# Spectral mixing with the weights as stationary 32-column tiles and a block-diagonal spectrum moving, and an inverse height transform in four 32-row tiles

## The reference

```python
xf = jnp.fft.rfft2(x, norm='forward')
w1 = jax.lax.complex(w1_real, w1_imag)
w2 = jax.lax.complex(w2_real, w2_imag)
top = jnp.einsum('bixy,ioxy->boxy', xf[:, :, :hm0, :hm1], w1)
bot = jnp.einsum('bixy,ioxy->boxy', xf[:, :, -hm0:, :hm1], w2)
out_fft = out_fft.at[:, :, :hm0, :hm1].set(top)
out_fft = out_fft.at[:, :, -hm0:, :hm1].set(bot)
return jnp.fft.irfft2(out_fft, s=(h, w), norm='forward')
```

## Time and profile before

| | |
|---|---|
| median of 3 runs | 598.17 us (598.06 to 601.45) |
| the profiled execution | 597.12 us, its span 595.3 us |
| PE busy | 552.4 us (93%), 9988 matmuls and 9988 weight loads |
| DVE, ACT, POOL busy | 346.0 (58%), 302.6 (51%), 115.1 us (19%) |
| mean granted clock of PE | 0.966 of full speed |
| transfers | 41.55 MB, 27.49 MB read from HBM |

### The profile page before, as it was taken

One profiled execution on the slowest core, in us unless ns is written; L12 is line 12 of the kernel. 1 busy time (PEld: TensorE's weight loads), 2 busy tenths in 40 slices (PEclk: granted clock), 3 DMA queues, 4 the chain that ended last, 5 costly groups with the idle time before them and its releaser, 6 DMA issues.

```text
span 595.3 us, 22931 instructions
## 1 busy us (share of the span) xinstructions
PE 552.4 (93%) x9988; PEld 500.4 (84%) x9988; DVE 346.0 (58%) x813; ACT 302.6 (51%) x838; POOL 115.1 (19%) x240
## 2 busy tenths in 40 slices
PE   8988988999999899986999999979999999987997
PEld 8978888999998797686999988868999999986873
DVE  3657989544435953784555445435555554568726
ACT  4546989553348610364444444424445777667200
POOL 4000000000016000000333333473332034372000
PEclk9999989999999797997999999979999999998979
DMA  9830765060000000000000012340000144600007
GB/s 354 350 141 2 284 233 196 2 254 30 1 2 1 2 2 20 0 2 1 4 4 3 5 26 70 98 101 4 4 4 4 26 78 76 107 10 1 2 3 282
DMA packets 50251, 41.55 MB, mean 70 GB/s; under 512 B 44998, under 2 KB 45126, under 8 KB 48934
## 3 DMA queue, kind: packets, MB, share of 16 engines
q1 hardware_dynamic: 49304, 38.51, 20.0%
q0 software_dynamic: 704, 1.18, 0.9%
q10 hardware_dynamic: 144, 0.39, 0.2%
HBM read 27.49 MB, written 4.19 MB: 53 GB/s over the span
## 4 chain that ended last, share of the span: by engine, by line
PE 75%; DVE 14%; POOL 4%; ACT 4%; issue 2%; DMA 0%; SPq 0%; POOLq 0%; DVEq 0%; ACTq 0%
PE PS L739 39%; DVE RB L971 5%; PE PS L708 5%; PE PS L473 4%; PE PS L658 3%; PE PS L602 2%; PE PS L572 2%; PE PS L551 2%; PE PS L558 2%; PE PS L452 2%; PE PS L527 2%; POOL RCD L393 2%; POOL RE L390 2%; PE PS L632 2%; PE PS L482 2%
## 5 line engine op out<-in xcount | busy, mean ns | idle before, releaser
L739 PE MATMUL PS<-RE,conv_sb 128*64 128x64 f32 x6048 | 231.2, 230 | 4.4 <-DVE RE L1109 4.0
L739 PEld LDWEIGHTS PS<-RE,conv_sb 128*64 128x64 f32 x6048 | 209.9, 139 | 25.7 <-DVE RE L1109 4.7
L864 ACT COPY PS<-convb_sb 128x64 f32<-128x64 f32 x504 | 108.2, 215 | 112.9 <-DVE RE L1121 98.8
L1121 DVE SCALAR_TENSOR_TENSOR RE<-PS,RCD 128x64 f32<-128x64 f32 x252 | 56.7, 225 | 58.1 <-PE PS L739 50.0
L402 POOL COPY RCD<-RE 128x128 f32<-128x128 f32 x126 | 37.0, 294 | 156.3 <-DVE RE L1121 156.2
L1121 DVE SCALAR_TENSOR_TENSOR RE<-PS,RE 128x64 f32<-128x64 f32 x126 | 32.7, 259 | 28.3 <-PE PS L739 25.9
L802 ACT COPY RB<-PS 32x256 f32<-32x256 f32 x64 | 42.3, 661 | 6.9 <-PE PS L511 6.2
L971 DVE COPY RB<-PS 32x256 f32<-32x256 f32 x64 | 42.1, 658 | 5.2 <-PE PS L511 4.3
L1121 DVE SCALAR_TENSOR_TENSOR RE<-PS,RB 128x64 f32<-128x64 f32 x126 | 28.4, 225 | 28.1 <-PE PS L739 28.1
L527 PE MATMUL PS<-RE,RB 128*64 128x64 f32 x1024 | 32.5, 224 | 7.7 <-DVE RCD L980 3.7
L473 PE MATMUL PS<-warm 128*128 128x128 bf16 x468 | 35.5, 244 | 3.9 <-DVE warm L892 1.4
(11 more groups left out here) (118 smaller groups left out, 769.6 us busy)
## 6 DMA issues: line engine op xcount, KB each, us to landing
RE<-wspec SPq DMA_DIRECT2D x8, 2048.0 KB, 8.9
RA<-x_in SPq DMA_DIRECT2D x8, 512.0 KB, 7.5
RCD<-x_in SPq DMA_DIRECT2D x1, 4096.0 KB, 13.4
out<-RA SPq DMA_DIRECT2D x8, 512.0 KB, 2.7
RCD<-RB SPq DMA_DIRECT2D x58, 64.0 KB, 2.6
RE<-RCD SPq DMA_DIRECT2D x32, 80.0 KB, 2.4
conv_sb<-conv_w SPq DMA_DIRECT2D x1, 768.0 KB, 20.0
w_sb<-w SPq DMA_DIRECT2D x2, 264.0 KB
```

Source lines behind the costliest of these rows:

```text
L739: m = pe.matmul(conv_bank(s, u, c)[o:o + OC], conv_sb[:, s, d, o:o + OC], prev, start=False, stop=(d == 2), skip_group_check=True)
L864: act.copy(banks_of, convb_sb[:, s:s + 1].unsqueeze(2).to_broadcast([P, c1 - c0, n])).then_inc(s_seed, 1)
L1121: dve.scalar_tensor_tensor(out=state[:, state_slot(s, u), b0:b1, 1:1 + HO], in0=conv_bank(s, u, c), scalar=0.0, in1=row_at(SRC[s], s, q, u ...
```

## The change

The roles in `mix` are exchanged. The weights are now stationary: for every kx and for real and imaginary part (w) a tile of 128 rows (4 ky x 32 input channels) and 32 columns (output channels). The spectrum moves: XB holds for each kx three planes of 32 columns (minus imaginary, real, imaginary), block-diagonal over the four ky, and a matmul takes two neighbouring planes, 64 columns. The two matmuls of a kx add up in PSUM, so that the complex product comes out whole. Four kx go to four column tiles (j), PSUM partitions 32 j. A chunk has 128 matmuls where it had 64. Two banks hold a chunk's result where four did, and they alternate between chunks; DVE drains one, ACT the other, into V in RC. The two slots of XB lie in RB and RD; POOL zeroes 6144 columns of each, the second after six groups of `dft_w` have read RD.

`spread` on each engine has for two ky a copy of 32 x 1024 and a negated one of 32 x 512. Imtmp, the turning of separate products, the subtraction and addition are gone; 64 transposes turn V into VT in RA, drained by ACT and DVE in turn. `dft_h` works on 32 rows (16 of kx, real and imaginary) in four row tiles, one for each ky (q), each into its own bank, and adds over four j: 256 matmuls of 32 x 128 by 128 in four groups, where there were 64 of 128 x 128. Its table `inv_h` becomes a parameter of its own (128 x 4 x 128, in the last 512 columns of RB), loaded as an eighth one. The drains of `dft_h` alternate between DVE and ACT. The copies after the first transposes write RA in another order, and the weights are packed otherwise, in the same 2 MB per chunk. The reload of x waits for the 64 transposes.

The core of the diff:

```diff
-WCOLS = 2 * X8 * KYC * 2 * C
+XCOLS = H * 3 * KYC * B
+WCOLS = H * 2 * C
@@ sync
+            sp.dma_start(inv_h, invh).then_inc(s_par, 16)
...
-                    sp.wait_ge(s_mix, 4 * (c - 2))
+                    sp.wait_ge(s_mix, 2 * (c - 2))
...
-            sp.wait_ge(s_t0, NCH)
-            sp.wait_ge(s_t1, NCH)
+            sp.wait_ge(s_pt, NCH)
             sp.dma_start(RC, x_in).then_inc(s_xr, 16)
@@ gpsimd
-            pool.memset(RB[:, :], 0.0).then_inc(s_zero, 1)
+            pool.memset(RB[:, 0:XCOLS], 0.0).then_inc(s_zero, 1)
+            pool.wait_ge(s_ff, XCOLS // 1024)
+            pool.memset(RD[:, 0:XCOLS], 0.0).then_inc(s_zero, 1)
@@ tensor, mix
-                for k in range(4):
-                    if c >= 1:
-                        pe.wait_ge(s_md if k < 2 else s_ma, 2 * (c - 1) + k % 2 + 1)
+                for k in range(2):
+                    if c >= 2:
+                        pe.wait_ge(s_ma if k else s_md, c - 1)
                     for n in range(8):
...
-                            m = pe.matmul(o[:, x % 2, y],
-                                          XB[:, c % 2, x, 2 * y + a].rearrange("p r q b -> p (r q b)"),
-                                          WR[:, c % 3, a, x, y, :], start=True, stop=True)
+                        for w in range(2):
+                            for j in range(4):
+                                x = 4 * (8 * k + n) + j
+                                m = pe.matmul(PS[C * j:C * j + C, 4 + 2 * (c % 2) + k, 64 * n:64 * n + 64], WR[:, c % 3, x, w, :],
+                                              XB[c % 2][:, x, 1 - w:3 - w].rearrange("p r q b -> p (r q b)"),
+                                              start=(w == 0), stop=(w == 1))
@@ tensor, after the mixing
+                for b in range(B):
+                    m = pe.transpose(blk(product_slot(c), b), V_of_b[:, c, :, b], ident)
+                m.then_inc(s_pt, 1)
+            def dft_h(i):
+                pe.wait_ge(s_pta, 3 if i == 0 else 4)
+                pe.wait_ge(s_ptd, 3 if i == 0 else 4)
+                if i >= 2:
+                    pe.wait_ge(s_dra if i % 2 else s_drd, 1)
+                for c in range(4):
+                    for j in range(4):
+                        for q in range(KYC):
+                            rows = slice(C * q, C * q + C)
+                            m = pe.matmul(blk(PS[:, 4 * (i % 2) + q, :], c), VT[rows, i // 2, 4 * (i % 2) + c, j],
+                                          inv_h[rows, j, :], start=(j == 0), stop=(j == 3))
+                m.then_inc(s_df, 1)
@@ vector, spread (ACT the same for q = 2, 3)
-                for o, i in xb_pairs(c, 0):
-                    m = dve.tensor_copy(o, i)
+                for q in (0, 1):
+                    (o, i), (o_neg, i_im) = xb_pairs(c, q)
+                    dve.tensor_copy(o, i)
+                    m = dve.tensor_scalar(o_neg, i_im, -1.0, None, ALU.mult)
```

More of the change, by code:

```diff
@@ L27 @@
 NCH = KY // KYC
-X8 = H // 2 // Q
-WCOLS = 2 * X8 * KYC * 2 * C
+KXH = H // 4
+XCOLS = H * 3 * KYC * B
+WCOLS = H * 2 * C
 NF = BH * TOK
@@ L38, with build_kernel @@
 AX_X = mybir.AxisListType.X
-def build_kernel(nc, x_in, dft, wspec, conv_w, conv_b, gate_w, gate_b, w1, w2, b2, own, out):
+def build_kernel(nc, x_in, dft, invh, wspec, conv_w, conv_b, gate_w, gate_b, w1, w2, b2, own, out):
     with ExitStack() as ctx:
@@ L197, in t1_pairs @@
             g = j - G_T1
[L198 to L223, removed]
+            o = RA[:, :].rearrange("p (t b k c) -> p t b k c", t=BH, b=BL, k=KY)[:, g // 4, :, 8 * (g % 4):8 * (g % 4) + 8]
@@ L508, in spectrum @@
                     pe.wait_ge(s_xba, c - 1)
-                for bh in range(BH):
-                    for y in range(KYC):
-                        m = pe.matmul(blk(PS[:, 2 * (c % 2) + bh, :], y), blk(RA, bh * KY + c * KYC + y), fwd_h,
-                                      start=True, stop=True)
+                for b in range(B):
+                    m = pe.matmul(blk(banks(2 * (c % 2), 2), b), blk(RA, b * NCH + c), fwd_h, start=True, stop=True)
                 m.then_inc(s_f2, 1)
@@ L796, in spread @@
                 act.wait_ge(s_f2, c + 1)
-                if c == 0:
-                    act.wait_ge(s_zero, 1)
-                if c >= 2:
-                    act.wait_ge(s_mix, 4 * (c - 1))
-                for o, i in xb_pairs(c, 2):
-                    m = act.copy(o, i)
+                if c < 2:
+                    act.wait_ge(s_zero, c + 1)
+                else:
+                    act.wait_ge(s_mix, 2 * (c - 1))
+                for q in (2, 3):
+                    (o, i), (o_neg, i_im) = xb_pairs(c, q)
+                    act.copy(o, i)
+                    m = act.activation(o_neg, i_im, ACT.Copy, scale=-1.0)
                 m.then_inc(s_xba, 1)
@@ L808, in _ @@
                     spread(c + 1)
-                for k in (2, 3):
-                    act.wait_ge(s_mix, 4 * c + k + 1)
-                    act.copy(z_bank(c, k), PS[:, 4 + k, :]).then_inc(s_ma, 1)
-            for c in range(NCH):
-                act.wait_ge(s_t1, c + 1)
-                if c >= 2:
-                    act.wait_ge(s_comb, c - 1)
-                act.copy(imtmp[:, c % 2, :], banks(4 * (c % 2) + 2, 2)).then_inc(s_tmp, 1)
-            for first, pairs in ((0, t2_pairs), (8, t3_pairs)):
-                for g in range(8):
-                    act.wait_ge(s_tf, first + g + 1)
-                    for o, i in pairs(g):
-                        m = act.copy(o, i)
-                    m.then_inc(s_td, 1)
+                act.wait_ge(s_mix, 2 * c + 2)
+                o, i = z_pair(c, 1)
+                act.copy(o, i).then_inc(s_ma, 1)
+            for c in range(0, NCH, 2):
+                act.wait_ge(s_pt, c + 1)
+                o, i = t2_pair(c)
+                act.copy(o, i).then_inc(s_pta, 1)
+            for n in (1, 3):
+                act.wait_ge(s_df, n + 1)
+                for o, i in if2_pairs(n):
+                    m = act.copy(o, i)
+                m.then_inc(s_dra, 1)
+            for g in range(8):
+                act.wait_ge(s_tf, g + 1)
+                for o, i in t3_pairs(g):
+                    m = act.copy(o, i)
+                m.then_inc(s_td, 1)
             def experts(l):
```

138 lines of the change are left out of this document (56 added, 82 removed).

## The result

The kernel after takes 608.6 us (median of 4 runs, 607.34 to 612.9) against 598.3 us (4 runs, 598.06 to 601.45): 2.0% slower, the ratio 1.0204 with a 95% interval of 1.0153 to 1.0254. The forecast was 605.5 us. The profiled execution took 609.57 us, its span 607.8; for before these are 597.12 and 595.3, a difference of 12.45 us.

The account below looks back on a forecast made before the run. DVE's spread bounded the mixing before, PE the time after it; after the change PE's instruction supply would bind. Mixing ending at 128.8, then 7.1, 14.8 + 2.5 and 3.1 put L602 at 156.3: +8.3 on 597.1, 605.5 us; 8-in-10 range 588 to 629.

Parts of the forecast that it names:

- DVE bound the mixing and is freed: Mixing stage: DVE's spread copies and drains set the pace at 6.6 us a chunk; the change cuts them to 4.5 us.
- the third that I gave as a sign: Mixing stage, sign that the forecast is right: DVE stands idle for a third of the stage.
- Start of the mixing: First spread ends after 3.8 us, at 55.8 us, and mixing starts there instead of at 57.36.
- Four column tiles quarter a pass: Mixing matmuls: two tiles halve a pass, so four were taken to quarter it, to 14.5 ns, 3.7 us for 256.
- rival of tiles that gain nothing beyond two: Mixing passes stay at 31 ns: 614 us, or 628 us if row tiles too go only by twos; together chance 0.28.
- The program sets the pace: Mixing: instruction pieces arrive every 3.5 us, later behind loads; 10.5 us a loaded chunk (bounds 5.9 and 12.4), 73 us in all.
- 2 to 4 as the sign: Mixing, sign that the forecast is right: PE gaps marked issue of 2 to 4 us, always 254 visible instructions apart.
- the second rival: Mixing: running loads don't matter, pieces come every 3.5 us, mixing ends at 113.8; 590 us, chance 0.15.
- Transposes: After the mixing: 64 transposes at 0.11 us each take 7.1 us, to 135.9, with their drains hidden.
- Inverse transform over the height: 512 passes at 29 ns on four row tiles, 14.8 us, plus 2.5 for a piece made late by the reload of x.
- Tail: After the height transform: the last group's two ACT copies and first turned one stay exposed, 3.1 us, before L602 starts.
- The rival of a program that arrives in time: Mixing and after: PE runs at its own pace without waiting for instructions, 24 us earlier; 573 us, chance 0.17.

## Why the prediction was right, and by how much it was off

The forecast was +8.3 us at the first L591; the profiles show 160.18 - 147.96 = 12.2, and 0.3 after it. Step by step:

- **DVE bound the mixing and is freed.** Right: copies of 1.21 and 0.67 us and a drain of 0.69, against 1.23, 0.69 and 0.69 forecast. Its share of the chain falls from 58.8% (L971 and L980) to 0.8%. DVE stands idle for 58% of the stage; the third that I gave as a sign did not follow from my own 4.5 us a chunk, which is half of 73.
- **Start of the mixing.** Forecast 55.8, measured 56.66, 0.9 us late. From the spread's start to the first mix it was 3.7 us, against 3.8; the stages ahead of it ended 0.9 later, and in other runs of the same front the first mix starts between 55.6 and 56.7. I had taken the front as fixed.
- **Four column tiles quarter a pass.** The number is right: 15.5 ns against 14.5. Two tiles measured 28.7, so four halve it again. The 57 ns of one tile came from a row whose moving operand has 8 columns (L691, `128*32 128x8`), not 32 or 64 as in the rows beside it; no run has one tile with 64, so the quarter itself is not measured. The rival of tiles that gain nothing beyond two falls.
- **The program sets the pace.** This was the step that everything rested on, and it holds: 3.45 to 4.01 us for a piece without a load (forecast 3.5), with 1.3 or 2.0 us of work in it. Start of mix to start of mix, the five chunks behind a load took 12.7, 9.0, 11.0, 10.3 and 10.2 us, 10.6 on average, against 10.5; the others 6.9, 5.4 and 7.9 against 6, 7.5 and 7.0. The mixing took 73.4 against 73. Its gaps were 0.9 to 4.0 us, where I had named 2 to 4 as the sign. With 12.7 the first loaded chunk lay beyond my bound of 12.4. That the sum came out within 0.4 us is partly luck. By the second rival's sum my model gives 58 us without any effect of the loads, so it put the loads at 15 us; the run without them took 61.8, so the loads are worth 11.6. One term was 3.8 us too small, the other 3.4 too large. Nor did the model count the slower passes, and PE was busy 6.75 us longer than in the run without loads.
- **Transposes.** 7.4 us against 7.1.
- **Inverse transform over the height.** This is the term that was mis-sized: 19.8 us (137.41 to 157.17) against 17.3. At full clock four row tiles take what I said, 14.8: the run with two column tiles and no loads has the 512 passes in 14.88 us. In the kernel after the gaps were 2.99 + 0.17 us where I took 2.5, and the passes took 1.8 us more than 14.88, most of it behind the gap, where 275 passes needed 9.43 us, 34 ns each. The granted clock is 0.85 there (the window is below), and 275 passes at 29 ns over 0.85 are 9.4 us. I had seen the slow passes after a gap and counted nothing, because slower passes lie behind the fetch. Here PE's work and the supply are nearly equal, 3.7 us each, and nothing hides them. For the mixing the reason is not shown either: with split matmuls slow spectra did lengthen their pieces.
- **Tail.** 3.0 against 3.1.

The passes of the height transform behind the gap:

```profile
147.81:157.17 9.36, 9.36 (x275) 9.24 (x275) 2.35 (x2) 1.93 (x2) 0.00 (x0) 0.85 0.08 30
```

Together, with the 0.3 behind the first L591, 0.9 + 0.4 + 0.3 + 2.5 - 0.1 + 0.3 = 4.3; the profiles differ from the forecast by 4.15 (12.45 against 8.3), the same within rounding.

Of the 73.4 us of the mixing, 11.6 are due to the loads and 17 to the number of instructions, by the run without loads; 44.9 are PE's work. The rival in which running loads don't matter gave 590, and 594.3 was measured when they were taken away: it falls because they matter. Its size kept the 2.5 us for a piece that the reload of x makes late, which don't belong to it; without them it is 588, 6 us under the run. The rival of a program that arrives in time gave 573. Only the run with 291 instructions a chunk, half of the matmuls left out, comes near that state (564.9); with all instructions no run was free of the gaps while four tiles worked.

The Trainium skill (Runtime: NRT & Kernel Launch, section "Instruction fetch mechanics") calls the crossing from one 16 KB block to the next mostly hidden. The runs here say when: with 3.7 us of work in a piece there was no gap in 70 us, with 2.0 or 1.3 us there was one behind every piece that held mixing matmuls alone.

## What to carry to other kernels

Count instructions as well as busy time: with f32 matmuls of two passes each, 256 visible instructions of PE cost 3.5 to 4.0 us here however small they are, so tiling that makes a pass cheaper than 29 ns buys little by itself (2.6 us of 76 here). A large transfer that is issued while PE runs on short instructions delays its program (2 MB by up to 4 us of standing still); issue it in parts, each behind a step of the work. Where PE waits for its program, put its slow instructions there (56 transposes at 115 ns, 6.4 us of work, lengthened the mixing by 2.6).

## What the runs showed that was not expected

- The interval from piece to piece hardly depends on what is in it: 3.73 us with 1.28 and with 1.99 us of work in the rows shown, 3.8 and 3.6 on average. With longer gaps the granted clock falls (1.00, 0.88 and 0.68 in the mixing of the run without loads, of the kernel after, and of the run with split matmuls); a spectrum that takes 2.05 us takes 3.0 to 3.8 in all but two of those in the last two, and one of 3.78 us ran at a granted clock of 0.50, the 1.2 GHz level.
- While loads of 2 MB run, a strided copy of DVE, 32 x 256 elements written 2 KB apart, takes 658 ns instead of 619, and the copies with runs of eight elements take the same 1.21 us.
- One kernel's time varies more than its first runs showed: 19 runs of before, on another chip, went from 593.4 to 601.3 us, with mean granted clocks from 0.980 to 0.960. A gain of 0.4% needed a dozen runs, and its interval still touches no change.
